# Ternary feed-forward layer: two LayerNorm multiplications move from VectorE to GpSimd

## The reference, cut to what matters

```
def _layernorm(x, axis=-1, eps=1e-05):
    m = jnp.mean(x, axis=axis, keepdims=True)
    v = jnp.var(x, axis=axis, keepdims=True)
    return (x - m) / jnp.sqrt(v + eps)

def _L0_ffn_ref(x, w1, b1, w2, b2):      # w1 2048 x 512, w2 512 x 2048
    w1q = _bit_quant(w1)                 # -1, 0 or 1 by a threshold at half the mean size
    w2q = _bit_quant(w2)
    h = jnp.einsum('bsd,fd->bsf', x, w1q) + b1
    h = jax.nn.gelu(h, approximate=False)
    return jnp.einsum('bsf,df->bsd', h, w2q) + b2

    ...
    x = _layernorm(x + _L0_xattn_ref(...), axis=-1)
    x = _layernorm(x + _L0_ffn_ref(x, ...), axis=-1)
```

## Time and profile before

| what | value |
|---|---|
| median of 3 runs | 2038.5 us (2036.71 to 2039.0) |
| profiled execution, its own time | 2037.29 us |
| profiled execution, span from first to last instruction | 2035.5 us |
| mean granted TensorE clock | 0.994 |
| PE busy / DVE busy / ACT busy / POOL busy | 1979.3 / 1412.0 / 1226.4 / 688.5 us |
| the ternary stage's loop in the span | about 1107 to 1216 us, its first half up to about 1165 us |

### The profile page before, as it was taken

One profiled execution on the slowest core, in us unless ns is written; L12 is line 12 of the kernel. 1 busy time (PEld: TensorE's weight loads), 2 busy tenths in 40 slices (PEclk: granted clock), 3 DMA queues, 4 the chain that ended last, 5 costly groups with the idle time before them and its releaser, 6 DMA issues. The chain is left out here.

```text
span 2035.5 us, 31350 instructions
## 1 busy us (share of the span) xinstructions
PE 1979.3 (97%) x11032; PEld 1560.9 (77%) x11032; DVE 1412.0 (69%) x3154; ACT 1226.4 (60%) x3186; POOL 688.5 (34%) x689
## 2 busy tenths in 40 slices
PE   8999999999999999999998999999999999999998
PEld 5644788888888988888986895666656786666997
DVE  2397677777777676767666847776777668996555
ACT  2073688878787878888774444544534447772332
POOL 1300344544545454545431001343252102332442
PEclk9999999999999999999998999999999999999999
DMA  4033434242424243342332303333131330003200
GB/s 189 10 119 129 137 87 152 71 151 87 152 70 152 87 132 90 99 140 71 111 101 75 107 1 124 122 115 129 58 145 69 131 103 22 2 2 148 85 1 33
DMA packets 60173, 193.66 MB, mean 95 GB/s; under 512 B 9408, under 2 KB 28640, under 8 KB 56048
## 3 DMA queue, kind: packets, MB, share of 16 engines
q1 hardware_dynamic: 48496, 172.15, 25.0%
q10 hardware_dynamic: 9504, 8.50, 1.4%
q0 software_dynamic: 2016, 11.01, 1.3%
HBM read 171.75 MB, written 19.48 MB: 94 GB/s over the span
## 5 line engine op out<-in xcount | busy, mean ns | idle before, releaser
L988 PE MATMUL psum<-la_w_both,context 128*128 128x256 f32 (+1 forms) x1536 | 343.6, 380 | 0.0
L988 PEld LDWEIGHTS psum<-la_w_both,context 128*128 128x128 f32 (+1 forms) x1536 | 277.4, 184 | 44.9
L1465 POOL TENSOR_TENSOR norm_std<-room 128x400 f32<-128x400 f32 x75 | 70.4, 938 | 271.5 <-DVE room L1230 271.3
L944 PE MATMUL psum<-qa_xqf,qa_two 128*128 128x400 f32 x640 | 156.2, 372 | 2.3 <-PEq L60 2.3
L944 PEld LDWEIGHTS psum<-qa_xqf,qa_two 128*128 128x128 f32 x640 | 115.4, 191 | 7.4 <-issue 3.2
L3029 ACT ACTIVATE itp_w_q<-psum,it_nm 100x257 f32<-100x257 f32 (+1 forms) x256 | 101.7, 415 | 25.0 <-DVE it_nm L3058 24.2
L1458 POOL TENSOR_TENSOR room<-room,qa_inv 128x500 f32<-128x500 f32 x64 | 89.7, 1402 | 53.0 <-DMA qa_inv<-qa_std_rows 50.8
L1006 PE MATMUL psum<-qa_kxT,room 128*100 128x361 f32 x256 | 100.4, 474 | 4.0 <-ACT qa_kxT L1148 2.9
L1154 ACT ACTIVATE qa_prob<-psum,qa_nm 100x361 f32<-100x361 f32 x128 | 71.9, 562 | 48.0 <-DVE qa_nm L1319 47.5
L1154 ACT ACT_TABLE_LOAD x64 | 82.1, 1283 | 24.0 <-ACT qa_size L1172 18.2
L2568 POOL TENSOR_TENSOR gf_last_diff<-la_gf_what,la_gf_w 128x512 bf16<-128x512 bf16 x24 | 27.0, 1146 | 200.6 <-issue 164.4
(11 more groups left out here) (396 smaller groups left out, 5307.4 us busy)
## 6 DMA issues: line engine op xcount, KB each, us to landing
context<-in_context SPq DMA_DIRECT2D x70, 722.0 KB, 4.6
qa_inv<-qa_std_rows SPq DMA_DIRECT2D x64, 250.0 KB
qa_w_raw<-in_qa_w SPq DMA_DIRECT2D x8, 1536.0 KB, 15.4
la_gf_raw<-in_gf_w SPq DMA_DIRECT2D x16, 768.0 KB, 4.6
qa_piece<-in_tf_pieces ACTq DMA_DIRECT2D x64, 128.0 KB, 2.1
la_w_qt<-in_qa_o SPq DMA_DIRECT2D x8, 1024.0 KB, 6.8
gf_ternary<-la_gf_made POOLq DMA_DIRECT2D x7, 768.0 KB
gf_ternary<-keep POOLq DMA_DIRECT2D x7, 768.0 KB
```

The source lines that it names most:

```text
L944: mm = pe.matmul(psum[:, bank, 0:HALF], two[:, part, j, k, :], xqf[:, PART_XQ[j], k, (h % 2) * HALF:(h % 2 + 1) * HALF], start=(k == 0 and ...
L988: mm = pe.matmul(psum[0:rows, i // 2, (i % 2) * 256:(i % 2) * 256 + 256], ctxT[:, n % 2, k, t0:t0 + rows], kv_raw[:, s, k, :], start=(k == ...
```

## The change

The two multiplications leave DVE's loop. GpSimd, which had no block in this stage, gets one with the same two operations. Each waits for the semaphore `inv_ready`, which the quarter's reciprocal raises.

```
--- before.py
+++ after.py
@@ -1731,8 +1731,6 @@
                         nrm.center(dve, 1, j)
                     if not at and j in (7, 10):
                         nrm.invert(dve, 1, (j - 7) // 3)
-                    if not at and j in (13, 14):
-                        nrm.apply(dve, 1, j - 13)
                     if not at and j == FC - 1:
                         low_parts(1)
                     if at and j == 0:
@@ -1756,6 +1754,11 @@
                 dve.wait_ge(S_["last_mean"], i + 1)
                 dve.tensor_tensor(nrm.cen[:, :, tok], X[:, :, tok], last_mean_at(i).unsqueeze(1).broadcast_to([P, C, QUARTER]),
                                   ALU.subtract).then_inc(nrm.cen_ready, 1)
+
+        @block.gpsimd
+        def _(pool):
+            for i in range(2):
+                nrm.apply(pool, 1, i)
```

## The result

The changed kernel takes 2039.64 us (median of 20 runs) and the kernel before 2037.08 us (median of 20 runs taken beside them; the 2038.5 us ahead of the prediction was the median of the first three). The ratio is 1.0014 with a 95% interval of 1.0008 to 1.002, so 1.6 to 4.1 us slower. The forecast was 2.1 us slower, 2040.6 us. Run twice more, the changed kernel stood at 1.0009 [1.0001, 1.0018] and 1.0012 [1.0003, 1.0021]. Nineteen of the changed kernel's 20 executions lie from 2037.5 to 2041.75 us; the twentieth took 3406.47 us at a granted clock of 0.552, and the ratio leaves it out.

The account below looks back on a forecast made before the run. DVE was taken as tight in the layer's first half, with PE (97% busy) just behind. +3.30 us for blocks and -1.17 for operations removed gave +2.1, so 2040.6 us against the median of 2038.5; range 2037.2 to 2042.8.

Parts of the forecast that it names:

- Where DVE is tight and PE just behind: First half of the layer, 1141 to 1151 us: DVE busy 9.78 of 10 us, PE 9.01; later shifts pass on undiminished.
- What is removed: Two L225 of 0.90 us each leave DVE's loop; the last `down` of the half could start 1.17 us earlier.
- What is added on GpSimd: Two multiplications of 128 x 800, 1.88 us each, in GpSimd's idle time, so costing nothing by themselves.
- What it does to DVE: In the first half's loop, GpSimd and DVE exclude each other: DVE held 1.70 us, twice, 3.40 us.
- The full block for the whole instruction: At each GpSimd multiplication, the skill's wording: DVE blocked for all of 1.88 us; the prediction went by the rows instead.
- The sum: At the half's last `down`: +3.30 us for the blocks, -1.17 for the operations removed, +2.1 us.
- The sign by which PE's listed waits would add up to 3.3 us more: Expected in the changed profile: PE's waits behind the held DVE operation add up to 3.3 us more than before.
- No hold: Rival in the DVE loop: GpSimd does not hold DVE up, whole 1.17 us gained, 2037.3 us; chance 0.08.
- Some kinds not held: Rival in the DVE loop: L1693 and L1702 may run beside GpSimd, +0.4 us, 2038.9 us; chance 0.10.
- A fall of the clock by the stalls: Rival at PE's stalls behind the blocks: TensorE's clock falls, +3.7 us for one fall, +5.3 for two; chance 0.08.
- the bound that the prediction read from rows 8: For PE's stalls: the clock falls from a stall between 1.77 and 2.27 us on, or from two close together.
- That nothing behind 1170 us would change: After the layer's first half: nothing there changes its duration; the second half is the same, 2.1 us later.

Follow-up runs that it names:

- gated: The changed kernel, with GpSimd also waiting until DVE's next L1700 is done before multiplying: 2040.85 us, ratio 1.0016 to the kernel before.
- doubled: The changed kernel, with GpSimd doing each multiplication twice, the second behind a semaphore of the first: 2044.31 us, ratio 1.0031 to the kernel before.
- once_more: The changed kernel run a third time, with nothing altered: 2039.78 us, +2.3 us against the kernel before.
- left_out: The kernel before without the two multiplications, a one-column DVE memset raising the semaphore instead: 2036.14 us, ratio 0.9995.
- early_inverts: The kernel before, multiplications still on DVE, with both reciprocals moved from j = 7 and 10 to the end of j = 4: 2036.68 us, ratio 0.9991.
- early_pool: The kernel before, with both reciprocals at the end of j = 4 and the multiplications on GpSimd right behind them: 2036.31 us, ratio 0.9993.

## Why the prediction was right

**Where DVE is tight and PE just behind** held. DVE's holds reached PE, and the shift of 2.08 us passed whole through the second half to the next stage.

**What is removed.** 1.17 us by the chain hidden, Gelu, copy, L1725; left out alone, it measured 1.16. The prediction's rows show this chain in the second half, and that is where its 2.02 us came from. ACT's L1652, which waited 1.65 us for X, starts without a wait after, as forecast.

**What is added on GpSimd.** 1.88 us by the fit through two sizes of L462, with 1.70 and 2.52 as bounds. Where GpSimd did not wait, the record reads 1.92 and 1.91; beside L1725 it reads 2.11 and 2.12, which is some 0.2 us of waiting on top. I had expected near 2.2.

**What it does to DVE.** 1.70 us a hold, from an overlap of 0.13 us at each handover. Measured: 2.12 - 0.47 = 1.65 and 2.13 - 0.48 = 1.65, and it was L1691 that was held. The full block for the whole instruction, which the Trainium skill's wording gives ("SBUF — State Buffer", Who interferes with whom), would have had 1.88; the measured 1.65 is 0.26 us under the 1.91 that GpSimd's operation takes, so the rows were the better guide.

**The sum.** PE's delay at the L1606 that started at 1157.52 was put at 3.30 us; it now starts 53.23 us behind the mark instead of 49.99, so 3.24. Then 3.24 - 1.16 = 2.08 against 2.1 forecast. The sign by which PE's listed waits would add up to 3.3 us more was read too simply: those from 1141 to 1161 us grow from 1.60 to 3.88, by 2.28, and the rest of the delay lies in later starts of the groups behind a stall, which the timeline lists as no wait.

**The rivals.** No hold: excluded by the L1691 rows. Some kinds not held: excluded by L1702 in `gated` and L1693 in `doubled`. A fall of the clock by the stalls: it did not come between 1141 and 1170 us (1.00), and it did in `doubled`. I had counted one stall of 1.5 us for each quarter; they come as 0.80 and 1.11 with eight matmuls between. But the bound that the prediction read from rows 8, between 1.77 and 2.27 us, does not stand. Ahead of the L173 at about 1103 us PE stands 2.26 to 2.28 us in all twelve profiles of this case. In eight of them the matmuls behind take 4.3 to 4.6 us, in four (`once_more`, `left_out`, `doubled`, `early_inverts`) 2.92, at a granted clock of 1.00. And at 1866 us the clock fell behind 1.06. So the length of the last stall does not decide alone. That no fall came behind the change's stalls rests on three profiles of the changed kernel and not on a bound, and the chance of 0.08 was not worked out from one.

**What was off** is the time to start from. Three runs gave 2038.5 for a median that twenty put at 2037.08, so the forecast of 2040.6 lies 1.0 us over the 2039.64 measured, though the difference between the kernels was forecast 0.5 us too small by the medians (2.1 and 2.56) and right by the trace. The range held both. That nothing behind 1170 us would change failed in two of the changed kernel's three profiles, at 1866 and at 1859 us; the third, without it, shows that the shift does not bring it about each time.

## What to carry to other kernels

An engine that is free is not free of charge. In these runs, GpSimd's elementwise work on SBUF took nearly its own duration (1.65 of 1.91 us) out of a DVE that works on SBUF back to back, so moving 0.90 us off DVE cost DVE 1.65. Look in the trace for DVE operations that last much longer than their quickest, beside a GpSimd operation, before you move anything there. Give GpSimd the stretches in which DVE is idle or runs an operation that goes on beside it, as the reciprocal did here, and before that fill DVE's own idle time with DVE's own work.

## What the runs showed of the hardware

- When both engines are released by one semaphore, GpSimd can come first: in `gated` its record starts 0.04 us after DVE's, and it was DVE that was held, for 1.76 us.
- DVE's reciprocal of 128 x 200 and a GpSimd multiplication ran side by side: 2.67 us for two in `early_pool` as in `early_inverts`, where GpSimd is idle.
- A GpSimd memset ran beside a tensor_tensor with two SBUF inputs (0.77 us, its ordinary time) and held a tensor_scalar (0.76 instead of 0.48 us).
- The granted clock fell behind stalls of 2.61 and 2.41 us in `doubled`, not behind pairs of 0.80 and 1.11 in the changed kernel. Behind one and the same stall of 2.27 us at about 1103 us it fell in eight profiles of twelve, and PE's first L1593 came 4.24 to 4.25 us behind the start of L173 either way, since DVE's L1708 was not ready sooner. Behind an idle time of 1.06 us at about 1865 us it fell in one profile of the changed kernel and not in another, for 1.5 us. With a kernel of 2037 us, an effect of 2 us is therefore read in the trace's local distance, which repeated to 0.01 us, before it is read in the time.
